# A three-phase decoder layer on one core: codes of h transposed by DMA, down products two tiles late, wq and wk split in halves, x treated tile by tile

## The chip, the cores and the metric

One core of a Trainium2 chip runs the whole program. The metric is the device time of one execution in microseconds; the time of before is the median of three runs. Engines: PE is TensorE, DVE VectorE, ACT ScalarE, POOL GpSimd, SP the queue that issues most DMAs.

## What is computed

Four sequences of 512 tokens, 512 features, float32. Three blocks, each on a layer norm of x and added back to x:

```python
x = x + attn(layernorm(x))                 # 16 heads of 32, window of 128 keys and 4 sinks
x = x + xattn(layernorm(x), token ids, c)  # expert e of 4 by id // 6250: silu(xn c_e^T) * (xn c_e^T) c_e^T
h = silu(bit_linear(xn, w_gate)) * bit_linear(xn, w_up)
x = x + bit_linear(rms_norm(h, ln_weight), w_down)
# bit_linear: activations rounded to codes of 8 bits per row (127 / max|row|), weights to -1, 0, 1
```

The hidden width F of the last block is 2048.

## The kernel before

`program` runs three phases one after the other: `attention_phase`, `expert_phase`, `ffn_phase`. Every engine has a hand-written stream of instructions, and semaphores are the only order between engines. Within an engine everything runs in the order written.

**Start of the attention phase.** SP loads x of batch 0 in four tiles, then wq, wk, wv, wo whole (1 MB each), then biases. Products of float32 are made from an upper part (rounded to fp32r) and a lower part of both operands, three matmuls each. ACT makes upper parts (`weight_hi`, `x_hi`), DVE lower ones (`weight_lo`, `x_lo`). DVE runs the statistics of the four x tiles, then all variances, POOL one power for all (`rstds`), DVE four `normalize`, `weight_lo` of q, four `x_lo`, `weight_lo` of k and v. PE transposes the four tiles, then waits for `w_lo_ready` and the last `x_lo` and makes `project("Q0")`, K0, Q1, K1, the counts of the routing, the first scores, V0 to V2. The routing of tokens to experts is a chain of small DVE steps (`then`), which stands in one piece before the first `v_of`. The attention units follow in a fixed order.

**Expert phase.** 19 tiles of 128 routed tokens. Before the loop PE transposes tiles 0 and 1; the loop makes z, the gate, the transposes of the product and y.

**Feed-forward phase** (lines 1361 to 1691). 16 tiles of 128 tokens, the hidden width in FC = 4 chunks of 512. For tile t: PE `transpose_x` (codes of x), `gate_up(t, c)` (4 gate and 4 up matmuls into one of two banks each), ACT `gate_of` (silu), DVE `hidden` (h), POOL `weighted` (hw = h times ln_w), ACT `squares` (two halves), DVE `top_of` (maxima, two halves), `sum_squares`, `scale_h`, then `quantize_h(t)` in two halves, which writes the codes to `hq_big`. PE turns the codes by `transpose_h(t, g)` (4 groups of 4 transposes into the banks `hT_ps`), ACT `hqT_of(t, g)` copies each group to `hqT` in bf16, and PE makes `down(t, g)`, 16 matmuls into the single bank `y_ps`. DVE's `y_of(t)` scales and adds them to x, SP stores.

The order on PE in iteration t: gate_up 0, 1, transpose_x(t+1), gate_up 2, transpose_h(t-1, 0), gate_up 3, the other three groups of transposes and the four of down(t-1). `down(t, 0)` waits until y_of(t-1) has emptied `y_ps`:

```python
if g == 0 and inside(t - 1):
    pe.wait_ge(y_ready, t)
```

DVE begins iteration t with

```python
if inside(t - 1):
    quantize_h(t - 1)
if inside(t - 2):
    y_of(t - 2)
```

and then `quantize_x(t+1)` and `hidden(t, 0)`.

## Time and profile before

| | us |
|---|---|
| runs, median of 3 (lowest, highest) | 821.5 (819.59, 821.88) |
| the profiled execution, its own time | 822.49 |
| its span, first to last instruction | 820.7 |
| PE busy, share of the span | 757.3 (92%) |
| DVE busy | 591.2 (72%) |
| ACT busy | 475.8 (58%) |
| POOL busy | 278.1 (34%) |
| mean granted clock of PE | 0.981 |

The profile is of one execution. The time holds 1.8 us beside the span. A row of the timeline gives start, length, engine, line, what is written from what, and in brackets the gap before it with what ended the gap. Matmuls overlap, so the issue time of a group is the distance to the next start. PEclk is the granted clock as a share of 2.4 GHz.

### The profile page before, as it was taken

What the parts mean: (1) busy time and instruction counts of PE and PEld (TensorE: products, weight loads), DVE (VectorE), ACT (ScalarE), POOL (GpSimd) and SP (SyncE); (2) the same over time, 40 slices, a digit from 0 to 9 for tenths busy, and PEclk for the clock granted to TensorE, in tenths of its full rate; (3) what the DMA queues carried; (4) which work ended last, traced back from release to release, by engine and by line L of the source; (5) the groups of instructions that cost most, each with busy time, mean ns of one, the idle gap of its engine ahead of it and who ended that gap; (6) DMA issues with size and microseconds to landing.
All of it is one profiled execution on the core that took longest, in us unless ns stands there. A gap on an engine that the chain in (4) does not pass through costs nothing. (4 is left out here: it accounts for less than half of the span.)

```text
span 820.7 us, 14537 instructions
## 1 busy us (share of the span) xinstructions
PE 757.3 (92%) x5390; PEld 522.8 (64%) x5390; DVE 591.2 (72%) x1090; ACT 475.8 (58%) x1053; POOL 278.1 (34%) x279
## 2 busy tenths in 40 slices
PE   3997999999999999999978699999958999999997
PEld 2774777777777777777756578888723444444443
DVE  6875766886668866676666468888628888888874
ACT  4355666766667666776555144444415677667664
POOL 1001204213142131314455334442115455455442
PEclk9998999999999999999999899999989999999999
DMA  9110103104031141303310375553130111110001
GB/s 317 43 53 13 41 28 103 53 26 156 26 104 36 44 143 37 105 27 122 111 53 1 129 276 183 183 191 116 39 136 21 39 40 52 40 39 26 27 14 39
DMA packets 23749, 66.28 MB, mean 81 GB/s; under 512 B 3904, under 2 KB 3904, under 8 KB 22017
## 3 DMA queue, kind: packets, MB, share of 16 engines
q1 hardware_dynamic: 18224, 48.83, 17.3%
q0 software_dynamic: 5456, 16.53, 5.8%
q8 instruction: 45, 0.74, 0.4%
q14 instruction: 24, 0.19, 0.1%
HBM read 52.71 MB, written 13.39 MB: 81 GB/s over the span
## 5 line engine op out<-in xcount | busy, mean ns | idle before, releaser
L506 ACT ACTIVATE probs<-s_ps,neg_max 128x512 f32<-128x512 f32 (+2 forms) x256 | 152.3, 610 | 19.4 <-DVE neg_max L660 17.7
L660 DVE TENSOR_REDUCE neg_max<-s_ps 128x2 f32<-128x1024 f32 (+2 forms) x128 | 124.5, 1015 | 38.2 <-PE s_ps L859 37.8
L879 PE MATMUL pT_ps<-ident,probs 128*128 128x128 f32 x832 | 113.8, 277 | 10.3 <-DVE probs L681 9.1
L518 ACT ACTIVATE probs<-pT_ps 128x512 f32<-128x512 f32 x96 | 57.4, 598 | 100.0 <-PE pT_ps L879 99.7
L879 PEld LDWEIGHTS pT_ps<-ident,probs 128*128 128x128 f32 x832 | 92.8, 142 | 25.2 <-DVE probs L681 11.4
L1404 POOL TENSOR_TENSOR hw<-h,ln_w_sb 128x512 f32<-128x512 f32 x64 | 80.8, 1274 | 82.1 <-DVE h L1532 82.1
L681 DVE COPY probs<-pT_ps 128x512 f32<-128x512 f32 x112 | 76.7, 685 | 36.8 <-PE pT_ps L879 36.4
L802 PE MATMUL side_ps<-w_hi 128*128 128x512 f32 x176 | 73.3, 416 | 2.6 <-DVE w_lo L583 2.6
L1641 PE MATMUL gate_ps<-w_tern,xqT 128*128 128x512 bf16 x256 | 66.7, 383 | 6.4 <-DVE h L1532 5.6
L1451 ACT ACTIVATE f_gate<-gate_ps,gu_scale 128x512 f32<-128x512 f32 x64 | 43.6, 683 | 46.0 <-PE gate_ps L1641 46.0
L802 PE MATMUL side_ps<-w_hi,w_lo 128*128 128x512 f32 x176 | 69.3, 394 | 0.0
L802 PE MATMUL side_ps<-w_lo,w_hi 128*128 128x512 f32 x176 | 69.2, 393 | 0.0
L1641 PE MATMUL up_ps<-w_tern,xqT 128*128 128x512 bf16 x256 | 66.6, 383 | 0.0
L1659 PE MATMUL f_y_ps<-w_tern,hqT 128*128 128x512 bf16 x256 | 63.6, 386 | 0.8 <-DVE v_next L1574 0.8
L383 POOL TENSOR_TENSOR aT_hi<-norm,one_col 128x512 fp32r<-128x512 f32 x15 | 15.6, 1040 | 125.0 <-DVE norm L672 86.6
L1532 DVE SCALAR_TENSOR_TENSOR h<-up_ps,gu_scale,f_gate 128x512 f32<-128x512 f32 x64 | 47.5, 748 | 13.9 <-ACT f_gate L1451 10.5
L901 PE MATMUL pv_ps<-probs,v_sb 128*32 128x256 f32 (+1 forms) x896 | 54.0, 379 | 0.1
L506 ACT ACTIVATION_READ_ACCUMULATOR probs<-s_ps,neg_max 128x1 f32 x256 | 52.8, 206 | 0.0
L375 POOL TENSOR_TENSOR norm<-rinv,one_col 128x512 f32<-128x512 f32 x16 | 16.7, 1041 | 101.0 <-DVE rinv L667 100.9
L1443 ACT ACTIVATE hqT<-hT_ps,minus_offset 128x512 bf16<-128x512 f16 x64 | 42.1, 682 | 6.8 <-PE hT_ps L1651 6.8
L1641 PEld LDWEIGHTS up_ps<-w_tern,xqT 128*128 128x128 bf16 x256 | 25.3, 99 | 30.8 <-issue 1.1
L1641 PEld LDWEIGHTS gate_ps<-w_tern,xqT 128*128 128x128 bf16 x256 | 22.9, 98 | 33.3 <-DVE h L1532 9.5
(239 smaller groups left out, 1661.0 us busy)
## 6 DMA issues: line engine op xcount, KB each, us to landing
w_piece<-w_ffn SPq DMA_DIRECT2D x24, 512.0 KB
w_stage<-w_ffn SPq DMA_DIRECT2D x12, 1024.0 KB
xres<-x POOLq DMA_DIRECT2D x4, 1024.0 KB, 5.8
xn<-x SPq DMA_DIRECT2D x12, 256.0 KB, 2.8
xn<-x SPq DMA_DIRECT2D x3, 1024.0 KB
x<-xres POOLq DMA_DIRECT2D x3, 1024.0 KB, 4.8
xn<-c SPq DMA_DIRECT2D x2, 1024.0 KB, 6.2
v_next<-c SPq DMA_DIRECT2D x2, 1024.0 KB, 6.2
```

The lines of the kernel that those rows point to most:

```text
L506: nc.scalar.activation(weights[qt][:, h, at:at + width(qt)], s_ps[:, h, 0:width(qt)], ACT.Exp, bias=neg_max[:, qt % 2, h:h + 1], accum_out ...
L518: nc.scalar.activation(out, turned_p, ACT.Identity).then_inc(slot_copied[0], 1)
L660: nc.vector.tensor_reduce(neg_max[:, qt % 2, 2 * s:2 * s + 2], s_ps[:, 2 * s:2 * s + 2, 0:width(qt)], AX.X, ALU.max, negate=True).then_inc ...
L681: nc.vector.tensor_copy(weights[qt][:, :, a:z], pT_ps[:, 1, :].rearrange("p (h n) -> p h n", h=GH))\
L802: last = nc.tensor.matmul(out, lt, r, start=(first and n == 0), stop=(final and n == len(terms) - 1))
L879: last = nc.tensor.transpose(pT_ps[:, k % 2, h * P:h * P + P], weights[qt][:, h, a:z], ident[:])
L901: last = nc.tensor.matmul(pv_ps[HD * h:HD * h + HD, to], v_sb[:, slot, f:f + HD], p, start=first, stop=final, tile_position=(0, HD * h))
L1404: nc.gpsimd.tensor_tensor(hw[:, t % 2, c, :], h[:, t % 2, c, :], ln_w[:, c * CHK:c * CHK + CHK], ALU.mult)\
L1451: nc.scalar.activation(gate[:, c % 2, :], gate_ps[c % 2][:], ACT.Silu, scale=gu_scale[:, t % 2, 0:1])\
L1532: nc.vector.scalar_tensor_tensor(h[:, i, c, :], up_ps[c % 2][:], gu_scale[:, i, 1:2], gate[:, c % 2, :], ALU.mult, ALU.mult).then_inc(h_re ...
L1641: last = nc.tensor.matmul(out[:], xqT[:, t % 2, k, :], weights[:, k, cols], start=(k == 0), stop=(k == DK - 1))
L1659: last = nc.tensor.matmul(y_ps[:], hqT[:, k, :], down_w[:, k, :], start=(k == 0), stop=(k == FK - 1))
```

## The change

The feed-forward phase: the codes of h are no longer turned by PE, except for the last tile. ACT's `pack(t, n)` writes each half of the codes to the new tile `hq` in bf16, and SP issues a DMA transpose of each half (128x1024) from `hq` to one of two buffers of `hqT` (`turn`). The down products come LATE_DOWN = 2 tiles late and are spread: `down(t-2, c)` behind `gate_up(t, c)`. `y_of` moves one iteration later. SP issues the turns of tile t ahead of the store of tile t-2. `pack(t, n)` waits for both turns of tile t-1, `quantize_h(t)` for `pack` of the half of tile t-1, and a turn for the down products of tile t-2.

The start: wq and wk are loaded and split in two halves of columns in the order q0, k0, v, q1, k1, o; tid is loaded after the biases. Statistics, power and normalising run tile by tile, `x_lo` in between. `first_query` makes Q0 with all upper products first, so that it starts with the upper part of q0 and x alone. The route chain is cut into four pieces, one behind each unit of the first group; POOL loads the residual before it waits for the route. In the expert phase the second transposes of x come behind the first z. The last four stores of attention go out on SP (0, 2) and ACT (1, 3).

```diff
+WEIGHT_PARTS = ("q0", "k0", "v", "q1", "k1", "o")
+LATE_DOWN = 2
...
-                weight_hi(0, "q")
-                for t in range(TT):
-                    x_hi(-1, t, s_ps[:, t, :])
-                weight_hi(1, "k")
-                weight_hi(2, "v")
+                x_hi(-1, 0, s_ps[:, 0, :])
+                x_hi(-1, 1, s_ps[:, 1, :])
+                weight_hi(0)
+                x_hi(-1, 2, s_ps[:, 2, :])
+                x_hi(-1, 3, s_ps[:, 3, :])
+                for i in (1, 2):
+                    weight_hi(i)
...
-                pe.wait_ge(side_left, nth(-1, "X3"))
                 whole = list(range(DK))
-                pe.wait_ge(w_lo_ready, 1)
-                project("Q0", side_ps[:], whole).then_inc(side_done, 1)
+                pe.wait_ge(side_hi, TT)
+                first_query().then_inc(side_done, 1)
...
+                def first_query():
+                    cols = slice(0, P)
+                    for n, (w, x, done, number) in enumerate((("hi", xT_hi, w_hi_ready, 1), ("hi", xT_lo, side_left, TT),
+                                                              ("lo", xT_hi, w_lo_ready, 1))):
+                        pe.wait_ge(done, number)
+                        for k in range(DK):
+                            last = nc.tensor.matmul(side_ps[:], (w_hi if w == "hi" else w_lo)["q"][:, k, cols], x[:, k, :],
+                                                    start=(n == 0 and k == 0), stop=(n == 2 and k == DK - 1))
+                    return last
...
+                v_of(-1, 0, v_banks[0], v_sb)
+                weight_lo(5)
+                for t in (1, 2):
+                    v_of(-1, t, v_banks[t], v_sb)
+                for qt, route_part in enumerate((tiles_needed, slots_given, slots_addressed, experts_of_tiles)):
+                    unit(0, 0, qt, False)
+                    route_part()
...
                     expert_product(z_ps[:], xT_hi[:, s % 2], xT_lo[:, s % 2], first).then_inc(z_ready, 1)
+                    if s == 0:
+                        transpose_x(1)
...
-                for t in range(TILES):
+                def turn(t):
+
+                    for n in range(HALVES):
+                        sp.wait_ge(hq_packed, t * HALVES + n + 1)
+                        if n == 0 and inside(t - 2):
+                            sp.wait_ge(y_summed, t - 1)
+                        sp.dma_start_transpose(hqT[:, t % 2, n * FK // HALVES:(n + 1) * FK // HALVES, :],
+                                               hq[:, n * HALF:n * HALF + HALF]).then_inc(h_turned, 16)
...
+                for t in range(TILES + LATE_DOWN):
+                    if inside(t) and t != TILES - 1:
+                        turn(t)
+                    if inside(t - LATE_DOWN):
+                        store(t - LATE_DOWN)
...
+                def pack(t, n):
+                    cols = slice(n * HALF, n * HALF + HALF)
+                    act.wait_ge(hq_ready, t * HALVES + n + 1)
+                    if inside(t - 1):
+                        act.wait_ge(h_turned, t * HALVES * 16)
+                    nc.scalar.activation(hq[:, cols], hq_code[:, cols], ACT.Identity, bias=minus_offset[:]).then_inc(hq_packed, 1)
...
                     gate_of(t, 0)
                     gate_of(t, 1)
+                    if before:
+                        pack(t - 1, 0)
...
+                    if before:
+                        pack(t - 1, 1)
                     squares(t, 0)
-                    if before:
-                        hqT_of(t - 1, 0)
                     gate_of(t, 3)
-                    if before:
-                        hqT_of(t - 1, 1)
-                        hqT_of(t - 1, 2)
                     squares(t, 1)
-                    if before:
-                        hqT_of(t - 1, 3)
...
                     if inside(t - 1):
                         quantize_h(t - 1)
-                    if inside(t - 2):
-                        y_of(t - 2)
+                    if inside(t - 1 - LATE_DOWN):
+                        y_of(t - 1 - LATE_DOWN)
...
                 quantize_h(TILES - 1)
-                y_of(TILES - 2)
-                y_of(TILES - 1)
+                for t in range(TILES - 1 - LATE_DOWN, TILES):
+                    y_of(t)
...
                 def down(t, g):
-                    pe.wait_ge(hqT_ready, t * FC + g + 1)
+                    if t == TILES - 1:
+                        pe.wait_ge(hqT_ready, g + 1)
+                    else:
+                        pe.wait_ge(h_turned, (t + 1) * HALVES * 16)
                     if g == 0 and inside(t - 1):
                         pe.wait_ge(y_ready, t)
...
+                    for c in range(FC):
+                        gate_up(t, c)
+                        if c == (1 if inside(t - 1) else 2) and inside(t + 1):
+                            transpose_x(t + 1)
+                        if inside(t - LATE_DOWN):
+                            down(t - LATE_DOWN, c)
+                for t in range(TILES - LATE_DOWN, TILES - 1):
+                    for g in range(FC):
+                        down(t, g)
```

PE before, from the last chunk of a steady tile to the first of the next (f_y_ps is `y_ps`):

```order
L1641 MATMUL gate_ps<-w_tern,xqT 128x512 x4
L1641 MATMUL up_ps<-w_tern,xqT 128x512 x4
L1651 MATMUL hT_ps<-f_ident,hq_big 128x128 x8
L1659 MATMUL f_y_ps<-w_tern,hqT 128x512 x4
L1651 MATMUL hT_ps<-f_ident,hq_big 128x128 x4
L1659 MATMUL f_y_ps<-w_tern,hqT 128x512 x12
L1641 MATMUL gate_ps<-w_tern,xqT 128x512 x4
L1641 MATMUL up_ps<-w_tern,xqT 128x512 x4
```

PE in the change at the same place, with the semaphores that a row waits for:

```order
L1714 MATMUL gate_ps<-w_tern,xqT 128x512 [waits h_ready]
L1714 MATMUL gate_ps<-w_tern,xqT 128x512 x3
L1714 MATMUL up_ps<-w_tern,xqT 128x512 x4
L1735 MATMUL f_y_ps<-w_tern,hqT 128x512 [waits h_turned]
L1735 MATMUL f_y_ps<-w_tern,hqT 128x512 x3
L1714 MATMUL gate_ps<-w_tern,xqT 128x512 [waits h_ready,xqT_ready]
L1714 MATMUL gate_ps<-w_tern,xqT 128x512 x3
L1714 MATMUL up_ps<-w_tern,xqT 128x512 x4
L1735 MATMUL f_y_ps<-w_tern,hqT 128x512 [waits f_y_ready,h_turned]
L1735 MATMUL f_y_ps<-w_tern,hqT 128x512 x3
L1714 MATMUL gate_ps<-w_tern,xqT 128x512 [waits h_ready]
```

Of the transposes and the down products that stood between the last chunk and the next tile one group of down is left. The next group, one chunk later, is the first of a tile and waits for `y_ready` (f_y_ready), and the gate products of chunk 1 stand behind it.

DVE in the change, beginning of iteration 10:

```order
L1642 TENSOR_SCALAR hq_big<-hw,h_mul 128x1024 [waits hq_packed,hq_step]
L1642 TENSOR_SCALAR hq_big<-hw,h_mul 128x1024 [waits hq_packed]
L1647 SCALAR_TENSOR_TENSOR v_next<-f_y_ps,y_scale,v_next 128x512 [waits y_summed]
L1599 TENSOR_SCALAR xq_big<-f_xn,x_inv 128x512 [waits xq_transposed,xq_step]
L1605 SCALAR_TENSOR_TENSOR h<-up_ps,gu_scale,f_gate 128x512 [waits up_summed,f_gate_ready]
```

The y of tile 7 stands behind the two halves of codes, as in the kernel before, where at this place it was the y of tile 8; the halves now wait for `pack` instead of PE's transposes.

DVE at the start of the program, before:

```order
L567 BN_AGGR bn_mv<-bn_st 128x2
L569 TENSOR_SCALAR var_eps<-bn_mv 128x1 [waits stats_done]
L573 TENSOR_SCALAR xn<-xn,bn_mv,rstd 128x512 [waits rstd_ready] x4
L578 SCALAR_TENSOR_TENSOR w_lo<-probs,w_hi 128x2048 [waits w_hi_ready]
L583 TENSOR_TENSOR w_lo<-s_ps,w_hi 128x4x128 [waits side_hi] x4
L578 SCALAR_TENSOR_TENSOR w_lo<-probs,w_hi 128x2048 [waits w_hi_ready]
```

and in the change:

```order
L591 BN_AGGR bn_mv<-bn_st 128x2 [waits stats_step]
L593 TENSOR_SCALAR var_eps<-bn_mv 128x1 [waits stats_done]
L597 TENSOR_SCALAR xn<-xn,bn_mv,rstd 128x512 [waits rstd_ready]
L608 TENSOR_TENSOR w_lo<-s_ps,w_hi 128x4x128 [waits side_hi]
L597 TENSOR_SCALAR xn<-xn,bn_mv,rstd 128x512 [waits rstd_ready]
L608 TENSOR_TENSOR w_lo<-s_ps,w_hi 128x4x128 [waits side_hi] x2
L603 SCALAR_TENSOR_TENSOR w_lo<-probs,w_hi 128x4x256 [waits w_hi_ready]
```

The last x tile's normalising and the lower parts of x are interleaved, and the lower part of q (now 256 of 512 columns) comes behind three of the four x tiles instead of ahead of them.

## Rows read from the trace of the kernel before

**Rows 1.** The page's busy times: us, share of the span, instructions of each engine.
```profile
PE 757.3 (92%) x5390; PEld 522.8 (64%) x5390; DVE 591.2 (72%) x1090; ACT 475.8 (58%) x1053; POOL 278.1 (34%) x279
```

**Rows 2.** Busy time by stretch: stretch, us, each engine's busy us, PEclk, DMA share, GB/s.
```profile
638.92:651.05 12.13, 11.87 (x69) 5.65 (x68) 10.63 (x24) 8.32 (x14) 6.23 (x7) 1.00 0.12 45
...
796.65:820.70 24.05, 18.05 (x97) 8.45 (x95) 12.05 (x25) 9.77 (x16) 5.59 (x5) 0.93 0.09 33
```

**Rows 3.** PE's timeline in one steady tile: start, us, line, out<-in, gap before and its end.
```profile
711.72 1.03 PE L1641 MATMUL gate_ps<-w_tern,xqT 128*128 128x512 bf16 x4
...
715.93 1.04 PE L1641 MATMUL gate_ps<-w_tern,xqT 128*128 128x512 bf16 x4 [0.26 <-DVE h L1532]
...
717.67 0.39 PE L1651 MATMUL hT_ps<-f_ident,hq_big 128*128 128x128 f16 x4
717.89 1.03 PE L1641 MATMUL gate_ps<-w_tern,xqT 128*128 128x512 bf16 x4
...
719.62 0.61 PE L1651 MATMUL hT_ps<-f_ident,hq_big 128*128 128x128 f16 x8
```

**Rows 4.** DVE's timeline in the same stretch.
```profile
711.75 0.15 DVE L1551 TENSOR_REDUCE h_top<-hw_max 128x1 f32<-128x2 f32 x1
...
712.74 1.42 DVE L1569 TENSOR_SCALAR hq_big<-hw,h_mul 128x1024 f32<-128x1024 f32 x2
714.07 0.75 DVE L1574 SCALAR_TENSOR_TENSOR v_next<-f_y_ps,y_scale,v_next 128x512 f32<-128x512 f32 x1
...
720.16 0.75 DVE L1532 SCALAR_TENSOR_TENSOR h<-up_ps,gu_scale,f_gate 128x512 f32<-128x512 f32 x1 [0.32 <-ACT f_gate L1451]
...
722.38 0.15 DVE L1543 TENSOR_REDUCE h_ss<-h_sq 128x1 f32<-128x2 f32 x1 [0.48 <-ACT sq_junk L1459]
...
722.64 1.21 DVE L1538 TENSOR_REDUCE hw_max<-hw 128x1 f32<-128x1024 f32 x1
723.88 0.15 DVE L1551 TENSOR_REDUCE h_top<-hw_max 128x1 f32<-128x2 f32 x1
```

**Rows 5.** ACT's timeline in the same stretch.
```profile
721.20 1.05 ACT L1459 ACTIVATE sq_junk<-h 128x1024 bf16<-128x1024 f32 x1
...
722.24 0.68 ACT L1443 ACTIVATE hqT<-hT_ps,minus_offset 128x512 bf16<-128x512 f16 x1
```

**Rows 6.** ACT's timeline at the start of the program.
```profile
10.85 1.91 ACT L471 ACTIVATE w_hi<-probs 128x2048 fp32r<-128x2048 f32 x1 [8.76 <-DMA probs<-wq]
```

**Rows 7.** PE's timeline in tile 1 of the feed-forward phase.
```profile
629.87 0.40 PE L1651 MATMUL hT_ps<-f_ident,hq_big 128*128 128x128 f16 x4 [1.26 <-DVE hq_big L1569]
631.26 1.81 PE L1641 MATMUL gate_ps<-w_tern,xqT 128*128 128x512 bf16 x4 [0.99 <-DVE h L1532]
632.86 1.91 PE L1641 MATMUL up_ps<-w_tern,xqT 128*128 128x512 bf16 x4
634.57 0.72 PE L1651 MATMUL hT_ps<-f_ident,hq_big 128*128 128x128 f16 x8
```

**Rows 8.** DMA issues: out<-in, queue, operation, count, KB each, median us to landing.
```profile
y<-xn SPq DMA_DIRECT2D x8, 256.0 KB, 2.0
...
probs<-wq SPq DMA_DIRECT2D x1, 1024.0 KB, 8.2
```

**Rows 9.** Busy time by stretch, columns as above, in tile 1.
```profile
632.00:634.00 2.00, 2.00 (x6) 0.76 (x5) 1.60 (x4) 2.00 (x4) 1.65 (x3) 0.50 0.00 0
```

**Rows 10.** SP's queue at the first small copies inside SBUF.
```profile
40.16 2.88 SPq L281 DMA_DIRECT2D v_sinks<-v_sb  x4
```

**Rows 11.** PE's timeline at the start: first projection, first unit of the first group.
```profile
17.54 0.80 PE L802 MATMUL side_ps<-w_hi 128*128 128x512 f32 x1 [2.61 <-DVE w_lo L583]
...
40.92 0.51 PE L851 MATMUL s_ps<-k_hi,q_hi 32*128 32x512 f32 x4 [1.20 <-DVE v_sb L603]
```

**Rows 12.** DVE's timeline at the start: the lower parts of wq and x.
```profile
12.79 2.29 DVE L578 SCALAR_TENSOR_TENSOR w_lo<-probs,w_hi 128x2048 fp32r<-128x2048 f32 x1 [0.29 <-ACT w_hi L471]
15.00 2.48 DVE L583 TENSOR_TENSOR w_lo<-s_ps,w_hi 128x512 fp32r<-128x512 f32 x4
```

More of the change, by code:

```diff
@@ L141, in attention_phase @@
         side_ps = ps("side_ps", [P, SEQ])
[L143 removed]
+        w_loaded = [sem(f"w{n}_loaded") for n in WEIGHT_PARTS]
         bias_loaded, wide_bias_loaded, biases_ready = sem("bias_loaded"), sem("wide_bias_loaded"), sem("biases_ready")
@@ L259, in attention_phase, with last_rows, part_columns @@
         stage = {"q": weights[0], "k": weights[1], "v": v_next, "o": xres}
+        def last_rows(t):
+            return x1[(BATCH - 1) * SEQ + t * P:(BATCH - 1) * SEQ + t * P + P, :]
+        def part_columns(part):
+            half = part[1:]
+            return slice(int(half) * D // 2, (int(half) + 1) * D // 2) if half else slice(0, D)
         with nc.Block() as block:
@@ L387, in split @@
                         .then_inc(attn_split, 1)
-                rstds(0)
-                pool.wait_ge(list_cleared, 16)
-                pool.wait_ge(route, ROUTE_STEPS)
-                pool.wait_ge(route_consts, 7)
+                for t in range(TT):
+                    first_rstd(t)
                 def list_tokens(b, g):
@@ L615, in then, with first_variance @@
                     dve.wait_ge(route, done[0])
-                for t in range(TT):
-                    stats_of(0, t)
-                dve.wait_ge(stats_step, TT)
-                for t in range(TT):
+                def first_variance(t):
+                    dve.wait_ge(stats_step, t + 1)
                     variance_of(0, t)
-                for t in range(TT):
-                    normalize(0, t)
-                weight_lo(0, "q")
-                for t in range(TT):
-                    x_lo(-1, t, s_ps[:, t, :])
-                weight_lo(1, "k")
+                stats_of(0, 0)
+                stats_of(0, 1)
+                first_variance(0)
+                first_variance(1)
+                stats_of(0, 2)
+                normalize(0, 0)
+                normalize(0, 1)
+                first_variance(2)
+                stats_of(0, 3)
+                first_variance(3)
+                normalize(0, 2)
+                x_lo(-1, 0, s_ps[:, 0, :])
+                normalize(0, 3)
+                x_lo(-1, 1, s_ps[:, 1, :])
+                x_lo(-1, 2, s_ps[:, 2, :])
+                weight_lo(0)
+                x_lo(-1, 3, s_ps[:, 3, :])
+                weight_lo(1)
                 dve.wait_ge(bias_loaded, 32)
@@ new lines, in slots_addressed, with experts_of_tiles @@
+                def slots_addressed():
+                    then(nc.vector.tensor_copy(slot[:], slot_f[:]))
+                    then(nc.vector.tensor_scalar(slot_tile[:], slot[:], P.bit_length() - 1, None, ALU.arith_shift_right))
+                    then(nc.vector.tensor_scalar(slot_row[:], slot[:], P - 1, None, ALU.bitwise_and))
+                    then(nc.vector.scalar_tensor_tensor(slot_at[:], slot_row[:], float(ROUTED_TILES), slot_tile[:], ALU.mult, ALU.add))
+                def experts_of_tiles():
+                    for e in range(1, EXPERTS):
+                        then(nc.vector.tensor_scalar(reached[:, e - 1, :], tile_no_f[:], first_tile[:, e:e + 1], None, ALU.is_ge))
+                    then(nc.vector.tensor_reduce(expert_f[:], reached[:].rearrange("p e t -> p t e"), AX.X, ALU.add))
+                    then(nc.vector.tensor_scalar(expert_of[:], expert_f[:], float(DK), None, ALU.mult))
@@ L767, in _ @@
-                then(nc.vector.tensor_reduce(expert_f[:], reached[:].rearrange("p e t -> p t e"), AX.X, ALU.add))
-                then(nc.vector.tensor_scalar(expert_of[:], expert_f[:], float(DK), None, ALU.mult))
-                assert done[0] == ROUTE_STEPS
-                dve.wait_ge(wide_bias_loaded, 32)
-                for t, bank in enumerate(v_banks):
-                    v_of(-1, t, bank, v_sb)
-                for qt in range(TT):
-                    unit(0, 0, qt, False)
+                dve.wait_ge(wide_bias_loaded, 32)
@@ L1658, in down @@
                     for k in range(g * DK, g * DK + DK):
-                        last = nc.tensor.matmul(y_ps[:], hqT[:, k, :], down_w[:, k, :], start=(k == 0), stop=(k == FK - 1))
+                        last = nc.tensor.matmul(y_ps[:], hqT[:, t % 2, k, :], down_w[:, k, :], start=(k == 0), stop=(k == FK - 1))
                     if g == FC - 1:
```

129 lines of the change are left out of this document (63 added, 66 removed).

## Prediction

> **What bounds the kernel now.** I read the page's busy shares, then busy time by stretch, then the timelines of TensorE (PE), VectorE (DVE) and ScalarE (ACT) over one tile of the last phase, and last the start of the program.
>
> PE is busy 92% of the span [rows 1]. Sixteen tiles of the feed-forward phase run from 614 to 821 us, and most of the change lies there. A tile in the steady stretch takes 12.13 us, of which PE is busy 11.87 and DVE 10.63, at full granted clock [rows 2]; tiles 2 to 14 repeat this to 0.01 us. In the timeline PE has one gap per tile, 0.26 us [rows 3]. So PE bounds this phase. The reader should see the second thing too: what PE does after the last gate and up products of a tile (issued from 717.89 to 719.62, [rows 3]). Until the next tile begins, 12.13 after 711.72, it transposes codes and makes the down products, 4.2 us of work that waits for nothing. That is the cover under which DVE does its serial work for the tile: last product h at 720.16, sum of squares at 722.38, row maximum at 722.64, the small scale steps, and then, as a tile earlier at 711.75 to 714.82, scale steps, codes and y, with xq and the first h of the next tile right behind [rows 4]. The cover just suffices: the 0.26 us gap is PE waiting for that first h.
>
> **The feed-forward phase, part by part.**
>
> *Removed:* the 16 transposes of codes per tile. A group of four moves PE's next start by 0.23 us (717.67 to 717.89, [rows 3]), so 0.9 us per tile for 15 tiles. On ACT, four copies of 0.68 us go (one shown [rows 5]) and two passes over 128x1024 come. No row shows this pass; the nearest is the squares pass of the same shape, 1.05 us [rows 5], the bounds are 0.68 and 1.91 (the 128x2048 copy of the start, [rows 6]), and I take 1.05. ACT has gaps in either case, so this costs nothing as long as PE or DVE is late by more.
>
> *Moved:* down products of tile t-2 now stand between the gate and up products of tile t, four groups in four places. So after the last gate and up products PE has only one group of down and then gate and up of one chunk of the next tile. Gate and up of a chunk take 1.73 us of issue (717.89 to 719.62), a group of four half of that, 0.86 [rows 3]. That is all PE has before it comes to the first down group, which waits for y_ps to be free, that is for `y_of(t-3)`. DVE issues that y behind both halves of `quantize_h(t-1)`, as before. Only the place on PE at which it is needed has moved forward, and the last h of the tile has moved back by 3.5 us relative to it.
>
> *The wait that appears:* from PE's last issue of up to h on DVE 0.2 us. From the start of h to the end of y: h 0.75, squares to h_ss 1.18 (721.20 to 722.38), h_ss to the maximum 0.26, maximum 1.24, scale steps 0.99, codes 1.33, y 0.75 [rows 4, 5], 6.5 us; with the 0.2 it is 6.7. (POOL's weighted product, 1.27 us, runs beside the squares and is no later.) PE has 0.86 + 1.73 = 2.6 us of work in that time. It stands still for 4.1 us, with gate and up of chunk 1 queued behind the waiting down group. After the wait comes three times down (2.6), three times gate and up (5.2) and the transposes of x (0.2), 8.0 us, to the next last issue. Period 6.7 + 8.0 = **14.7 us against 12.1**. DVE then has slack, and the wait for h(t,0) is hidden under the down group and chunk 1.
>
> *Sum without the clock:* twelve periods, tile 3 to tile 15, at +2.57 each: +30.8. Head: tile 2 starts 4.3 us earlier, since tile 1 has no down and no transposes behind it (its last up products end issuing at 634.57 [rows 7], tile 2 began at 638.92 [rows 2]), of which about 1.3 is lost to the first wait for h: -3. Tail: from the start of tile 15 before 24.05 us [rows 2]. Now 14.4 for the tile, codes ready and `y_of(13)` (which stands behind `quantize_h(15)`) done at 20.2, down of tile 14 3.5, y 0.9, down of tile 15 with its transposes 4.0, last y 0.9, store 2.0 [rows 8] and 0.7 of steps between them, 31.9; PE's idle 5.8 us in it costs as much clock as in [rows 7], +1.7: 33.6, so +9.6. Together **+37.4**.
>
> *The clock:* behind two gaps of 1.26 and 0.99 us the granted clock fell to 0.50, the 1.2 GHz level [rows 9], from about 631.3 to 634.6: gate and up took 3.31 us of issue (631.26 to 634.57) instead of 1.73 [rows 7], 1.6 lost. Each new stall of 4.1 us is longer than both of those gaps together. The work behind the stall is all on the new path, so each costs about 1.7 us. Thirteen stalls, tiles 3 to 15: **+22**. Bounds: nothing, and +32 if the low clock lasts 1.5 times as long, since a gap of 4.1 us is longer than those of [rows 7].
>
> *The DMA transposes:* two per tile, 128x1024 bf16 each (256 KB), on SP's queue between the stores. No row shows one. Lower bound: a 256 KB store lands in 2.0 us [rows 8]. Upper bound: 64 pieces of 16 rows, each at the queue time of a small copy inside SBUF, 0.72 us (2.88 for four, [rows 10]): 46 us. I take 3 to 5, nearest to the store, because the bytes and the one command are the same. Free of cost are up to 7.6 us per half: a period of 16.4 (14.7 and the clock) holds one pass and two halves in series before `pack` of the next tile, and the first down group that reads the result comes no sooner. SP's stores and loads behind them have six tiles of slack. The Trainium skill speaks both ways here: "Advanced Engine Details and Errata", X-Bar Transpose (TRN2), says such a transfer is as fast as a plain one, "VectorE: DVE Perf Modes", The three transpose paths, gives 1309 ns for one 128x128 block. By the first the sum stays as it is; eight such blocks in a row would be an estimated 10.5 us a half, which is the rival C below. No run here shows which holds.
>
> **The start and the seams.** PE's first projection started at 17.54, 2.61 us after its transposes, and waited for DVE [rows 11]: DVE had normalised all four x tiles, then split all of wq (from 12.79), then split x from 15.00 [rows 12]. ACT began with wq at 10.85, when it had landed, 8.2 us after its issue [rows 6, 8]. Now the last x tile, there since 7.5, goes through statistics 0.7, variance 0.4, power 0.6, normalising 0.5, queueing behind the others about 1, transposes 0.9, copy 0.6: PE starts the hi products at about 12.4, with half of wq landed before 10.85 and a split of half the columns (1.15). Gain 5.1 us. The parts of wk, wv and wo behind it are still there before their projections. The 1.20 us that PE waited before 40.92 [rows 11] goes too, but the routing steps that DVE did in one piece now stand between the units of the first group, 3.9 us in all; with the gaps that DVE has there I count +1.0 net of that 1.20. On POOL only waits move. In the expert phase PE takes the second transpose behind the first product: -0.6, the time of one such group; the last four stores on two queues: -0.3. Sum **-5**, bounds 0 and -8.
>
> **Total:** 37.4 + 22 - 5 = +54. The profiled execution took 822.49 us with a span of 820.7, so 877; the median of the runs is 821.5, 1 us less: **876**. What this kernel's measurement can tell from no change is about 0.3%, 2.5 us.
>
> **Rivals.**
> A, the forecast: the wait for y with the drops of the clock. For it: every term is a row, and the place of y behind the codes is in the order. 865 to 890.
> B, the wait for y, but the clock holds, since 10.6 us of work between stalls may suffice. For it: the 1.20 us gap of [rows 11] was followed by scores at their usual speed. Against it: [rows 7, 9], and 4.1 us is far longer. 822.5 + 37.4 - 5 - 1 = 854.
> C, the transposes are the bound: two halves in series and a pass, because `pack` of the next tile waits for both. It decides from 7.6 us a half. At 10 us a half, a value between those ends, the period is 21: 8.9 more on 13 or 14 tiles, +120, and the tail +10: about 945.
> D, faster: y comes in time and PE runs without gaps. Its tile would be 48 products at 0.216 and 0.2 for x, 10.6, but DVE's own 10.6 [rows 2] fills it as well; between 10.6 and 12.1 I take 11.2: 0.93 less on 13 tiles, -12, with the start -5: 804. It decides if the 6.7 us chain fits in PE's 2.6 us behind the last up products. The chain of [rows 4] speaks plainly against that; only an order of waits other than I read could bring it.
> E, the gains of the start and a shorter stall cancel: no change.
>
> **Chances.** A 0.68, B 0.14, C 0.10, D 0.06, E 0.02. The range 848 to 897 takes in A and B with the bounds of the clock (+10), of the start (+5, -3) and of the pass, and leaves out C and D. Faster 0.06, within 0.3% 0.02, slower 0.92.
>
> **What would show it.** Right: in the steady tiles one PE gap of about 4 us before f_y_ps, released by DVE's y (v_next or xn), the group gate_ps of chunk 1 behind it, the granted clock near 0.8 in that stretch, the period 16 to 17 us, and DVE's share falling. First PE projection near 12.4 us. Wrong: PE's gap released by a DMA (C), no gap (D), a gap with clock 1.00 (B), or a first projection not before 16 us.

## The result, and the profile after

| | before | after |
|---|---|---|
| runs, median of 4 (lowest, highest), us | 820.57 (819.59, 821.88) | 885.18 (883.97, 886.48) |
| ratio, 95% interval | | 1.0786 (1.0765 to 1.0808) |
| span of the profiled execution, us | 820.7 | 882.5 |

The change makes the kernel 7.9% slower. 876 us with a range of 848 to 897 was predicted, so the median lies 9 us over the forecast and inside the range. Between the two profiled executions (spans 820.7 and 882.5) the difference is 61.8 us, and the table at the end of this section divides it.

The page of the kernel after, busy time by engine (us, share of the span, instructions) and the granted clock in 40 slices. To compare with [rows 1]:

```profile
PE 768.5 (87%) x5150; PEld 516.9 (59%) x5150; DVE 591.5 (67%) x1092; ACT 472.2 (54%) x1025; POOL 280.4 (32%) x282
...
PEclk9989999999999999999989999998998897888798
```

No engine has much more to do than before: PE makes 240 matmuls fewer (5150 instead of 5390), and its 11 us more of busy time are slower groups, shown below. PE's share fell from 92% to 87%, DVE's from 72% to 67%. The time is in waiting, and from slice 31 on, in the feed-forward phase, PEclk shows mostly 8 and 7, where [rows 2] has 1.00.

PE's timeline in one steady tile of the kernel after (start, us, line, out<-in, count, gap before it and what ended it), to hold against [rows 3]:

```profile
766.14 1.02 PE L1735 MATMUL f_y_ps<-w_tern,hqT 128*128 128x512 bf16 x4 [4.21 <-DVE v_next L1647]
...
782.77 1.87 PE L1735 MATMUL f_y_ps<-w_tern,hqT 128*128 128x512 bf16 x4 [4.21 <-DVE xn L1647]
784.43 1.91 PE L1714 MATMUL gate_ps<-w_tern,xqT 128*128 128x512 bf16 x4
786.14 1.81 PE L1714 MATMUL up_ps<-w_tern,xqT 128*128 128x512 bf16 x4
787.79 0.39 PE L1703 MATMUL f_xT_ps<-f_ident,xq_big 128*128 128x128 f16 x4
...
794.92 1.03 PE L1714 MATMUL up_ps<-w_tern,xqT 128*128 128x512 bf16 x4
800.15 1.44 PE L1735 MATMUL f_y_ps<-w_tern,hqT 128*128 128x512 bf16 x3 [4.21 <-DVE xn L1647]
```

There is one gap of 4.21 us a tile, before the first down group (f_y_ps), ended by DVE. A row with this gap stands in every tile from 3 to 15, at 646.93 first and at 851.37 last, twelve periods later: 204.44 / 12 = 17.04 us a tile, against 12.13 in [rows 2]. Behind the gap the groups of four take 1.87 and 1.91 where they take 1.03 later. What DVE did in the stall, to hold against [rows 4]:

```profile
776.08 0.75 DVE L1605 SCALAR_TENSOR_TENSOR h<-up_ps,gu_scale,f_gate 128x512 f32<-128x512 f32 x1 [0.71 <-PE up_ps L1714]
...
778.05 0.15 DVE L1616 TENSOR_REDUCE h_ss<-h_sq 128x1 f32<-128x2 f32 x1 [0.24 <-ACT sq_junk L1535]
...
778.31 1.21 DVE L1611 TENSOR_REDUCE hw_max<-hw 128x1 f32<-128x1024 f32 x1
...
780.55 1.42 DVE L1642 TENSOR_SCALAR hq_big<-hw,h_mul 128x1024 f32<-128x1024 f32 x2
781.88 0.75 DVE L1647 SCALAR_TENSOR_TENSOR xn<-f_y_ps,y_scale,xn 128x512 f32<-128x512 f32 x1
782.54 0.48 DVE L1599 TENSOR_SCALAR xq_big<-f_xn,x_inv 128x512 f32<-128x512 f32 x1
...
788.06 0.75 DVE L1605 SCALAR_TENSOR_TENSOR h<-up_ps,gu_scale,f_gate 128x512 f32<-128x512 f32 x1 [4.31 <-PE up_ps L1714]
```

The chain reads as the prediction listed it: last h 776.08, h_ss 778.05, maximum 778.31, the scale steps, both halves of the codes 780.55, and only then y at 781.88 to 782.63, 0.14 before PE goes on at 782.77. DVE, once done with the next xq and h, waits itself 4.31 us for up_ps of chunk 1, which is queued on PE behind the stalled group.

Busy time by stretch (stretch, its length, busy time of PE, PEld, DVE, ACT and POOL with counts, granted clock, DMA share, GB/s):

```profile
766.14:782.77 16.63, 12.42 (x52) 5.40 (x53) 10.71 (x25) 8.06 (x12) 6.29 (x7) 0.84 0.28 65
784.00:788.00 4.00, 4.00 (x14) 1.53 (x13) 0.00 (x0) 1.62 (x2) 1.02 (x1) 0.54 0.00 0
646.93:851.37 204.44, 153.95 (x625) 64.72 (x626) 125.66 (x279) 96.16 (x143) 74.30 (x81) 0.84 0.25 57
```

From 784 to 788 the granted clock is 0.54, close to the 1.2 GHz level; over the twelve periods it is 0.84. The next rows are the pack pass on ACT, then the DMA transposes and a store among the DMA issues (count, KB, median us to landing):

```profile
786.38 0.69 ACT L1527 ACTIVATE f_gate<-gate_ps,gu_scale 128x512 f32<-128x512 f32 x1 [7.79 <-PE gate_ps L1714]
786.97 1.14 ACT L1520 ACTIVATE hq<-hq_big,minus_offset 128x1024 bf16<-128x1024 f16 x1
```

```profile
y<-xn SPq DMA_DIRECT2D x8, 256.0 KB, 2.3
...
hqT<-hq SPq DMA_TRANSPOSE x30, 3.1
```

The start, to hold against [rows 11], shows PE's first transposes, the second pair, the first projection, and the first gate product of the feed-forward phase (614.20 before).

```profile
6.56 1.94 PE L848 MATMUL s_ps<-ident,xn 128*128 128x128 f32 x8 [6.56 <-DVE xn L597]
8.83 2.17 PE L848 MATMUL s_ps<-ident,xn 128*128 128x128 f32 x8 [0.33 <-DVE xn L597]
11.68 2.07 PE L874 MATMUL side_ps<-w_hi 128*128 128x512 f32 x4 [0.69 <-ACT w_hi L493]
...
607.32 1.04 PE L1714 MATMUL gate_ps<-w_tern,xqT 128*128 128x512 bf16 x4 [0.78 <-ACT xqT L1508]
```

At the end stand the down products of tile 14 behind `y_of(13)`:

```profile
867.78 6.20 PE L1735 MATMUL f_y_ps<-w_tern,hqT 128*128 128x512 bf16 x16 [5.93 <-DVE v_next L1647]
```

With the starts of tiles 3 and 15 (651.05 and 796.65 before, 640.84 and 845.27 after) the 61.8 us between the spans split up without a rest:

| stretch | before | after | difference | forecast |
|---|---|---|---|---|
| start to first gate product of tile 0 | 614.20 | 607.32 | -6.9 | -5 |
| tile 0 to start of tile 3 | 36.85 | 33.52 | -3.3 | -3 |
| twelve tiles, 3 to 14 | 145.60 | 204.43 | +58.8 | +30.8 and 12 x 1.7 |
| start of tile 15 to the end | 24.05 | 37.23 | +13.2 | +9.6 and 1.7 |

### The profile page after: what moved, and what is told of

Same layout as the page of the kernel before. It is cut to its first block and busy times, and to the rows that moved or that the text cites. A ratio compares the mean times of both kernels' runs of the same rounds, so it can differ in the third digit from the quotient of the medians.

```text
span 882.5 us, 14098 instructions
## 1 busy us (share of the span) xinstructions
PE 768.5 (87%) x5150; PEld 516.9 (59%) x5150; DVE 591.5 (67%) x1092; ACT 472.2 (54%) x1025; POOL 280.4 (32%) x282
## 2 busy tenths in 40 slices
DMA packets 56482, 74.12 MB, mean 84 GB/s; under 512 B 35615, under 2 KB 37663, under 8 KB 54752
## 5 line engine op out<-in xcount | busy, mean ns | idle before, releaser
L1735 PE MATMUL f_y_ps<-w_tern,hqT 128*128 128x512 bf16 x256 | 74.2, 420 | 61.7 <-DVE xn L1647 33.7
L930 PEld LDWEIGHTS pT_ps<-ident,probs 128*128 128x128 f32 x832 | 92.6, 142 | 25.5 <-DVE probs L717 11.7
L1735 PEld LDWEIGHTS f_y_ps<-w_tern,hqT 128*128 128x128 bf16 x256 | 25.0, 105 | 96.8 <-issue 75.8
L1714 PE MATMUL gate_ps<-w_tern,xqT 128*128 128x512 bf16 x256 | 76.7, 428 | 4.2 <-DVE h L1605 3.3
L1714 PE MATMUL up_ps<-w_tern,xqT 128*128 128x512 bf16 x256 | 76.9, 429 | 0.0
L843 PE MATMUL side_ps<-w_hi 128*128 128x512 f32 x172 | 71.1, 413 | 0.0
L843 PE MATMUL side_ps<-w_hi,w_lo 128*128 128x512 f32 x172 | 67.3, 391 | 0.0
L843 PE MATMUL side_ps<-w_lo,w_hi 128*128 128x512 f32 x172 | 67.2, 391 | 0.0
L1714 PEld LDWEIGHTS up_ps<-w_tern,xqT 128*128 128x128 bf16 x256 | 27.9, 109 | 39.1 <-issue 15.5
L1714 PEld LDWEIGHTS gate_ps<-w_tern,xqT 128*128 128x128 bf16 x256 | 26.7, 106 | 40.9 <-issue 8.7
```

The costliest lines, as they stand in the source:

```text
L843: last = nc.tensor.matmul(out, lt, r, start=(first and n == 0), stop=(final and n == len(terms) - 1))
L930: last = nc.tensor.transpose(pT_ps[:, k % 2, h * P:h * P + P], weights[qt][:, h, a:z], ident[:])
L1714: last = nc.tensor.matmul(out[:], xqT[:, t % 2, k, :], weights[:, k, cols], start=(k == 0), stop=(k == DK - 1))
L1735: last = nc.tensor.matmul(y_ps[:], hqT[:, t % 2, k, :], down_w[:, k, :], start=(k == 0), stop=(k == FK - 1))
```

## The experiments

All times below are medians; the ratio is to runs of the kernel before on the same chip, with its 95% interval. Edits are against the kernel after unless said otherwise; they are shortened, with constants and some arguments written out or left out as `...`.

**1. The new front with the old feed-forward phase.** `ffn_phase` is that of before, all else that of after.

> The new start, attention and expert code with the feed-forward phase of before. Theory (the loss lies wholly in the feed-forward phase; the front gains what its first feed-forward product shows, 614.20 - 607.32 = 6.9 us): 820.6 - 6.9 = about 814 us, gap of 1.20 us before the first unit gone. Rival (part of the loss comes from the front, such as routing steps between the units, and the earlier start is given back by a wait for the routed rows or the weights later): 820 us or more.

815.55 us, ratio 0.9925 (0.9897 to 0.9953). PE's first gate product of the phase:

```profile
608.65 1.04 PE L1694 MATMUL gate_ps<-w_tern,xqT 128*128 128x512 bf16 x4 [0.78 <-ACT xqT L1492]
```

5.6 us earlier than before, and the period is again 12.13 (tile starts at 633.65, 645.78, 657.91). So the loss of the change lies wholly in the feed-forward phase, and the front by itself is a gain of 5.4 us by the medians, 3.9 to 8.5 by the interval. The front of the change gave 6.9 in its own profiled execution. In the eleven kernels with this front the phase starts between 606.12 and 610.21, and a difference of 1.3 us between two of them lies within that spread.

**2. The down products in one block again.** DMA transposes, pack passes and LATE_DOWN stay.

```diff
                     for c in range(FC):
                         gate_up(t, c)
...
-                        if inside(t - LATE_DOWN):
-                            down(t - LATE_DOWN, c)
+                    if inside(t - LATE_DOWN):
+                        for g in range(FC):
+                            down(t - LATE_DOWN, g)
```

> The changed kernel with the four groups of down products of tile t-2 in one block behind the last gate and up products of tile t, not spread between the chunks; DMA transposes kept. Theory (the spread took away TensorE's cover for VectorE's serial work): the wait for y goes, 4 x 0.86 = 3.4 us of cover come back, what is left is about 1.0 us for xq and 0.4 for the first h, period about 12.1, clock near 1.00, total 815 to 830 us. Rival 1 (the DMA transposes or the pack passes are the cost): no gain, about 885. Rival 2 (it is a matter of TensorE's work alone, which is 0.9 us a tile less than before): period 11.2, 805.

824.6 us, ratio 1.0039 (1.0017 to 1.0062). PE in a steady tile:

```profile
760.78 0.40 PE L1703 MATMUL f_xT_ps<-f_ident,xq_big 128*128 128x128 f16 x4 [1.16 <-DVE xq_big L1599]
761.43 1.04 PE L1714 MATMUL gate_ps<-w_tern,xqT 128*128 128x512 bf16 x4 [0.26 <-DVE h L1605]
...
765.11 3.40 PE L1735 MATMUL f_y_ps<-w_tern,hqT 128*128 128x512 bf16 x15
768.35 1.03 PE L1714 MATMUL gate_ps<-w_tern,xqT 128*128 128x512 bf16 x4
```

The wait for y is gone, with y in the same place on DVE. What is left is 1.16 for xq and 0.26 for h; the period is 12.35 (756.00 to 768.35) at full clock. So 60.6 us go with the spreading alone (885.18 - 824.6): the block of 3.4 us behind the last up products was the cover for DVE's serial chain. The DMA transposes do not carry the loss. Nor do they carry a gain here: PE has about 0.9 us a tile less to do and waits about that much longer. The 9 us over experiment 1 are 12 x 0.22 of the period and 6.5 of a longer end: tile 15 starts at 793.05 here and needs 30.5 us for its own work and two tiles' down products, against 24.05 [rows 2].

**3. The stall filled with products.** This takes the clock and the wait apart. The results of the added products are not used.

```diff
                     if g == 0 and inside(t - 1):
+                        if t < TILES - LATE_DOWN:
+                            for n in range(16):
+                                nc.tensor.matmul(hT_ps[0][:].bitcast(F32).rearrange("p k n -> p (k n)"),
+                                                 ident[:], gate_w[:, 0, 0:D], start=True, stop=True)
                         pe.wait_ge(y_ready, t)
```

> The changed kernel with 16 products of 128x128 by 128x512 into an idle bank (their result is not used) ahead of each wait for y, so that TensorE is busy for 16 x 0.216 = 3.5 of the 4.2 us of each stall. Theory (a stall costs the length of the wait and, through the clock, about 2.4 us more): the wait itself stays, the clock stays near 1.00, period 14.7 instead of 17.0, total 885 - 12 x 2.4 = about 856 us. Rival (the slow groups have another cause, such as the DMA transposes beside them; the clock in the records only goes with them): about 885, or more by what the products add.

858.92 us, ratio 1.0457 (1.0426 to 1.0488). PE at two waits, and the granted clock over ten periods:

```profile
768.41 1.04 PE L1739 MATMUL f_y_ps<-w_tern,hqT 128*128 128x512 bf16 x4 [0.67 <-DVE xn L1648]
...
779.00 3.62 PE L1736 MATMUL hT_ps<-w_tern,f_ident 128*128 128x512 bf16 x16
783.29 1.04 PE L1739 MATMUL f_y_ps<-w_tern,hqT 128*128 128x512 bf16 x4 [0.67 <-DVE xn L1648]
```

```profile
650.00:800.00 150.00, 142.64 (x674) 64.61 (x686) 107.58 (x242) 79.52 (x120) 63.79 (x71) 1.00 0.30 67
```

The wait ends no sooner: from where the filling begins (779.00), behind the last up products, to y (783.29) are 4.29 us, and the period is 14.88 (768.41 to 783.29). But the clock stays at 1.00, and 26.3 us are gone. So the forecast's two terms are shown apart: the wait costs 14.88 - 12.13 = 2.75 us a tile, the clock 17.04 - 14.88 = 2.16 us a tile.

**4. y ahead on VectorE.**

```diff
-                    if inside(t - 1 - LATE_DOWN):
-                        y_of(t - 1 - LATE_DOWN)
...
                     hidden(t, 3)
+                    if inside(t - LATE_DOWN):
+                        y_of(t - LATE_DOWN)
                     if inside(t + 2):
                         top_of_x(t + 2)
```

> The changed kernel with y of tile t-2 on VectorE right behind the last h of tile t, instead of behind both halves of the next codes; nothing else moved. Theory (TensorE waits because y stands behind the codes): the wait for y falls from 4.2 us to under 0.3; next late is xq of the next tile, still behind the codes, with a wait of about 1.7 us; period 12.3 without the clock, up to 14.1 with it, total 818 to 835 us. Rival (y is late because its down products or the transposed codes are late): the wait stays, about 885.

820.14 us (10 runs), ratio 0.9984 (0.9967 to 1.0000).

```profile
762.21 0.40 PE L1703 MATMUL f_xT_ps<-f_ident,xq_big 128*128 128x128 f16 x4 [1.72 <-DVE xq_big L1599]
...
774.69 0.40 PE L1703 MATMUL f_xT_ps<-f_ident,xq_big 128*128 128x128 f16 x4 [1.72 <-DVE xq_big L1599]
```

```profile
650.00:800.00 150.00, 129.79 (x619) 58.62 (x632) 125.33 (x279) 98.78 (x143) 74.55 (x82) 1.00 0.34 78
```

One call moved on DVE takes back 65 us. From 640 to 790 us PE waits for nothing but xq (20.6 us in all, 12 times), 1.72 a tile as expected, and the period is 12.48. The clock did not fall at these waits, so the total is the lower end of what was expected.

**5. A second PSUM bank for y**, orders as in the change. `down` and `y_of` take `y_bank(t)` in place of `y_ps`.

```diff
+        def y_bank(t):
+            return y_ps[:] if t % 2 or t == TILES - 2 else hT_ps[1][:].bitcast(F32).rearrange("p k n -> p (k n)")
...
-                    if g == 0 and inside(t - 1):
-                        pe.wait_ge(y_ready, t)
+                    if g == 0 and inside(t - 2):
+                        pe.wait_ge(y_ready, t - 1 if t < TILES - 2 else t)
```

> The changed kernel with the down products of even tiles in a second PSUM bank (one of hT_ps, idle until the last tile), orders as in the change. Theory (the wait is for the one y bank to be read, which nothing else needs so early): no wait for y though y stands where the change has it; next late is xq of the next tile behind codes and y, about 2.1 us a tile; period 12.9, total 826 us if the clock holds at such a gap as it did at 1.72 us, about 850 if it falls. Rival (the down group was late for another reason): the 4.2 us stay, 885.

829.45 us, ratio 1.0107 (1.0088 to 1.0126).

```profile
763.77 0.40 PE L1706 MATMUL f_xT_ps<-f_ident,xq_big 128*128 128x128 f16 x4 [1.93 <-DVE xq_big L1602]
```

The granted clock is 1.00 from 650 to 800 us here too. The wait for y disappears though y stands on DVE where the change has it. Experiments 2, 4 and 5 remove it in three independent ways (cover, order, bank), and each lands in its expected range or within 4 us of its number.

**6. The transposes taken twice in the change.** This tests how much slack they have. The counts that `pack` and PE wait for are doubled too.

```diff
-                        sp.dma_start_transpose(hqT[...], hq[...]).then_inc(h_turned, 16)
+                        for again in range(2):
+                            if again:
+                                sp.wait_ge(h_turned, ((t * HALVES + n) * 2 + again) * 16)
+                            sp.dma_start_transpose(hqT[...], hq[...]).then_inc(h_turned, 16)
```

> The changed kernel with each DMA transpose done twice, the second after the first has landed, so a half takes about 2 x 3.1 = 6.2 us. The prediction's step (free of cost up to 7.6 us a half in a period of 16.4 or more): 885 us, within 5, and the stall for y as before. Rival (two halves in series are on or near the path already at 3.1, or the pass of the next tile, which waits for both and holds up the gate behind it, becomes the bound below 7.6): up to 1.4 us more a tile, 900 us or more.

889.47 us, ratio 1.0840 (1.0822 to 1.0859). PE at the first down group of all and at one of a steady tile, and SP's queue in that tile:

```profile
634.89 1.89 PE L1739 MATMUL f_y_ps<-w_tern,hqT 128*128 128x512 bf16 x4 [5.13 <-DMA hqT<-hq]
...
787.74 1.86 PE L1739 MATMUL f_y_ps<-w_tern,hqT 128*128 128x512 bf16 x4 [4.21 <-DVE xn L1651]
```

```profile
775.33 8.75 SPq L1433 DMA_TRANSPOSE hqT<-hq  x4
```

In the steady tile nothing moved: 4.21 us for y. The 4.3 us more come from one wait of 5.13 for the transposes, at tile 2, where no stall for y precedes; in the change it is 0.48. The slack can be read too. One transpose holds the queue for 1.23 us and lands after 3.1, so the last of the four, issued by 784.08, landed at about 784.08 - 1.23 + 3.1 = 785.95, 10.6 after the first was issued; PE needed it at 787.74, 12.4 after. Two halves in strict series may thus take 6.2 us each, not 7.6.

**7. xq and the first h ahead of the codes**, on top of experiment 4. The first h of tile 0 moves ahead of the loop.

```diff
                     sum_squares(t)
                     top_of(t, 1)
+                    if t >= 1 and inside(t + 2):
+                        quantize_x(t + 2)
+                    if t >= 1 and inside(t + 1):
+                        hidden(t + 1, 0)
                     scale_h(t)
...
-                    if inside(t - 2) and inside(t + 1):
-                        quantize_x(t + 1)
-                    if t != 1:
-                        hidden(t, 0)
```

> e4_y_early, and on VectorE also xq of the tile after next and the first h of the next tile ahead of the scale steps and the codes. Theory (what TensorE waits for in e4, 1.72 us a tile, is xq behind the codes): that wait falls to about 0.3 us; but ScalarE still takes each pack pass in front of its gate and squares, waits there for the codes, and the last h and with it y come later: a wait for y of about 1.2 us; period 12.1 against 12.48, total about 815 us. Rival (VectorE's order was all that was wrong): period 10.8, 798 us.

814.92 us, ratio 0.9935 (0.9911 to 0.9960). PE's waits from 640 to 790 us, summed by what ended them (us, times, longest):

```profile
PE f_y_ps L1736 <- DMA hqT<-hq: 16.7, 13, 1.3
```

The total is the one expected, the reason is not. PE waits about 1.3 us a tile for the DMA transposes, not for y. ACT explains it:

```profile
745.11 1.15 ACT L1520 ACTIVATE hq<-hq_big,minus_offset 128x1024 bf16<-128x1024 f16 x1 [2.57 <-DVE hq_big L1642]
...
748.01 1.14 ACT L1520 ACTIVATE hq<-hq_big,minus_offset 128x1024 bf16<-128x1024 f16 x1
```

ACT stands 2.57 us at the first pack pass, since the codes now come later, with gate 2 and the second pack pass queued behind. The second half is packed at 749.15 and lands 3.1 later, at 752.3; PE's next down group starts at 752.35.

**8. ScalarE's order mended too**, on top of experiment 7.

```diff
                     if before:
-                        pack(t - 1, 0)
-                    if inside(t + 2):
-                        normalize_x(t + 2)
-                    if before and inside(t + 1):
-                        xqT_of(t + 1)
-                    gate_of(t, 2)
...
+                        if inside(t + 1):
+                            xqT_of(t + 1)
+                        pack(t - 1, 0)
+                        gate_of(t, 2)
+                        pack(t - 1, 1)
+                        if inside(t + 2):
+                            normalize_x(t + 2)
+                        gate_of(t, 3)
+                        squares(t, 0)
```

> e5_x_h_early, and on ScalarE xqT ahead of the first pack pass, the second pack pass behind gate 2, then xn, gate 3 and both squares passes. Theory (ScalarE's order is what is left, TensorE's own work 48 products and one group of transposes, 10.6 us, is next): no PE wait over 0.3 us in the steady tile, period 10.8, total about 798 us. Rival (VectorE, 10.7 us busy a tile, does not fit so closely): period 11.5, 807 us.

795.86 us, ratio 0.9694 (0.9677 to 0.9710): faster than both kernels, 25 us under before. The same place on PE in two tiles, and the busy times of eleven tiles:

```profile
741.67 0.39 PE L1707 MATMUL f_xT_ps<-f_ident,xq_big 128*128 128x128 f16 x4
...
752.49 0.39 PE L1707 MATMUL f_xT_ps<-f_ident,xq_big 128*128 128x128 f16 x4
```

```profile
645.00:765.00 120.00, 119.87 (x578) 52.78 (x577) 115.78 (x266) 90.41 (x133) 69.44 (x77) 1.00 0.38 91
```

The period is 10.82 us, PE is busy 119.87 of 120.00, and DVE 115.78: this is TensorE's own work, next to VectorE's limit.

**9. The transposes taken twice in that kernel.** The edit of experiment 6 on experiment 8.

> e6_act_order with each DMA transpose done twice, the second after the first has landed (as in e9_after_twice, about 6 us a half). Theory (the transposes are free in the change only because the stall for y makes its tile long; in a tile of 10.8 us two halves of 6 us and a pack pass of 1.1, which wait for one another, do not fit): the period goes to 13.5 us or more, PE waits released by the DMA transposes, total 830 to 880 us. Rival (the slack is larger than I count): 796 us as e6.

895.68 us, ratio 1.0908 (1.0859 to 1.0956), beyond the range expected.

```profile
705.55 1.89 PE L1743 MATMUL f_y_ps<-w_tern,hqT 128*128 128x512 bf16 x4 [6.22 <-DMA hqT<-hq]
...
723.63 1.89 PE L1743 MATMUL f_y_ps<-w_tern,hqT 128*128 128x512 bf16 x4 [4.68 <-DMA hqT<-hq]
```

```profile
711.80 1.14 ACT L1524 ACTIVATE hq<-hq_big,minus_offset 128x1024 bf16<-128x1024 f16 x1
```

```profile
712.97 8.79 SPq L1433 DMA_TRANSPOSE hqT<-hq  x4
```

Now PE waits 4.6 to 6.3 us a tile for the transposes and the period is 17 to 19 us. The rows on ACT and SP give the chain: 712.97 + 8.79 - 1.23 + 3.1 = 723.63, which is the very time at which PE goes on. I had counted two halves and a pack pass in a ring, 13.5 us, and that step was wrong. But the pack pass stands on ACT behind gate 1 and xqT, and both stand on PE behind the stalled down group, so the time from PE's start to the first pack pass (705.55 to 711.80, at the lower clock) is in the ring too.

**10. VectorE's new order with the transposes on TensorE.** Experiment 1 with the edit of experiment 7.

> e1_old_ffn (new front, feed-forward phase of before with transposes on TensorE and one block of down) with xq of the tile after next and the first h of the next tile ahead of the scale steps and codes on VectorE, as in e5. It asks what of e6's 795.9 us belongs to the DMA transposes and what to VectorE's order. Theory (with the order mended TensorE's own work bounds the tile, and it has four groups of transposes more, 0.9 us a tile): 48 x 0.216 + 5 x 0.225 = 11.5 us a tile against e6's 10.8, so 796 + 14 x 0.7 = about 806 us. Rival (the codes, now 1.2 us later, are late for TensorE's transposes, which stand only one tile behind): a new wait for hq_big, period 12 or more, 813 us or slower.

839.2 us, ratio 1.0226 (1.0189 to 1.0264): 24 us slower than experiment 1, against 806 expected. The rival's time, 813 or slower, holds; its reason, a wait for the codes, does not, since from 650 to 800 us PE waits only for h (10.6 us in all) and for the copies of transposed codes (10.1).

```profile
747.62 0.75 DVE L1585 SCALAR_TENSOR_TENSOR h<-up_ps,gu_scale,f_gate 128x512 f32<-128x512 f32 x1 [1.61 <-PE up_ps L1695]
```

```profile
741.49 0.38 PE L1705 MATMUL hT_ps<-f_ident,hq_big 128*128 128x128 f16 x4 [0.91 <-ACT hqT L1496]
...
752.37 1.04 PE L1695 MATMUL gate_ps<-w_tern,xqT 128*128 128x512 bf16 x4 [0.96 <-DVE h L1585]
...
755.41 0.38 PE L1705 MATMUL hT_ps<-f_ident,hq_big 128*128 128x128 f16 x4 [0.91 <-ACT hqT L1496]
```

DVE stands 1.61 us before the first h of the next tile, because here PE makes that tile's first up products only behind the block of down; scale steps and codes are queued behind it, and PE then waits 0.96 for an h and 0.91 for a bank of transposed codes; the period is 13.92 (741.49 to 755.41) against 12.13. The same move that gained 5 us in experiment 7 loses 24 here. So it cannot be said from these runs what the DMA transposes alone are worth; they and the late, spread down products make the order of experiment 8 possible, and no kernel that keeps the transposes on TensorE with another order was tried.

## Why the prediction was right, and where its sizes were off

**The wait for y: right.** There is one gap a tile before f_y_ps, of 4.21 us (4.1 forecast). It is ended by DVE's y behind the codes, and chunk 1 is queued behind it. Order, cover and bank each remove it (experiments 4, 2, 5). Its price was 14.7 - 12.13 = 2.57 a tile in the forecast and is 2.75 in experiment 3. PE's own work between two waits is 10.6 us as summed (768.41 to 779.00); the stall is 4.29 there for 4.1 in the forecast. Over twelve periods this makes 33.0 us against 30.8.

**The clock: right in kind, too small in size.** The forecast was 1.7 us a stall, and 2.16 was measured. The 1.7 came from [rows 7], where the low clock caught gate and up of one chunk, two groups (3.31 - 1.73 = 1.6 there, which the sum took as 1.7). Behind a gap of 4.21 us it catches up to three: those at 782.77, 784.43 and 786.14 take 5.02 us of issue where three groups take 2.59 at full clock, 2.4 lost, and that period is 17.38 (782.77 to 800.15); behind 766.14 the first group is fast, and that period is 16.63. Over twelve periods this makes 25.9 us instead of 20.4, the largest part of what the forecast was short by. The bound of 1.5 times the length, which the range took in, covers it.

**The tail: right, 2 us short.** The difference is +13.2 against +11.3. The prediction's terms for it add up to 32.2 us, not to the 31.9 that it gives, which is 0.3 of the 2. The gap before tile 14's down products is 5.93 us as forecast (5.8), but behind it all sixteen products ran in 6.20 us, where sixteen take 3.62 at full clock (the filling in experiment 3): 2.6 for the clock, not 1.7.

**The DMA transposes: right, by a narrower margin than stated.** They take 3.1 us from issue to landing in the change, within the 3 to 5 taken. The step that was wrong is the slack: 7.6 us a half was worked out from the whole period of 16.4, on the ground that the first down group comes no sooner than `pack` of the next tile. It comes sooner: PE's group starts at 782.77, the pass at 786.97. Experiment 6 shows 12.4 us for both halves, 6.2 each. It did not matter at 3.1. Of the two places in the Trainium skill, "Advanced Engine Details and Errata", X-Bar Transpose (TRN2), which has transposing DMAs as fast as plain ones, is the nearer: 3.1 us against 2.0 to 2.3 for a store of the same bytes is not equal but close. The 1309 ns that the Trainium skill has for one 128x128 block in "VectorE: DVE Perf Modes", The three transpose paths, would be an estimated 10.5 us for a half; eight blocks in one transfer took 3.1 here, 0.39 us each, and the measurement decides. No run here times a single block.

**The pack pass: right.** It took 1.14 against 1.05, and it is hidden in the change, since just ahead of it ACT waits 6.75 us for PE in one of the tiles read and 7.79 in the other.

**The start: right, a little more than forecast.** The first projection starts at 11.68 (12.4 forecast, though the steps listed for it add up to 12.2; 17.54 before), and between 11.7 and 12.5 in the eleven kernels with this front. At the first gate product of the feed-forward phase the gain is 6.9 us in the change and 5.6 in experiment 1, for -5 in the forecast. The gap of 1.20 us is gone, as forecast. What the routing steps cost between the units, +1.0 in the sum, was not measured by a run of its own; the one gap of PE there that grew, before the transposes of `sinks`, went from 2.17 us (63.33) to 3.00 (58.10).

**The rivals.** B (the clock holds) is what experiment 3 brought about; its 854 was 859. (Its sum keeps the tail's 1.7 for the clock, and the tail was not filled in experiment 3 either, so the two can be compared.) C (transposes bound) is what experiment 9 shows, but in a kernel without the stall for y and with transposes at 10.6 us a pair. D (no stall, 804) is what the change could have been: experiment 8, with a period of 10.82, went below its tile of 11.2, but only with y, then xq and the first h, and then ScalarE's order changed. The prediction's reason against D, that the chain of 6.7 us does not fit in 2.6 us of cover, was the one that counted.

## What to carry to other kernels

Moving work on the busy engine moves its cover too: before spreading a block between other work, read which serial chain runs under it and where its last result is now needed. When a transfer or a product is made a tile later, look at the order on every other engine again, since steps that once had to come first (here codes before y, xq and h) need not any more; and mend all engines, as half a reordering can cost more than none (experiment 10). Price a stall of TensorE at its length and at the slower groups behind it, if the granted clock falls there, and take the two apart by filling the stall with products that nobody uses.

## What was not expected of the hardware

- One gap a tile of 1.72 us (experiment 4) or 1.93 (experiment 5) left the granted clock at 1.00 over 150 us. In the kernel before, two slow groups at 0.50 followed a gap of 1.26 with one of 0.99 shortly behind [rows 7, 9], and slow groups followed the gaps of 4.21. One and the same gap of 2.1 us for xq in tile 2 was followed by groups of 1.03 in the change (634.56) and by groups of 1.29, 1.91 and 1.65 in experiment 4 (635.75). So the length of one gap alone does not tell whether the clock falls; what does was not settled.
- A DMA transpose of 128x1024 bf16 inside SBUF holds SP's queue for 1.23 us and lands after 3.1. With the new front alone (experiment 1) the program moves 24,804 packets, with 30 transposes 56,482 and with 60 (experiments 6 and 9) 88,163, so each makes about 1,056. The stores of y in the same queue took 2.3 us to land against 2.0.
- Adding 16 products of no use in each stall made the kernel 26 us faster than the change (experiment 3).
